# A two-layer graph network with a gated feed-forward block: how the two edge passes are drained into the stages behind them

## The chip, the cores and the metric

The kernel runs on one core of one Trainium2 chip, in one launch. The metric is device time in microseconds; a kernel's time is the median of its runs. One more execution of each kernel is profiled, and all rows below come from that one.

## The reference

`x` is [20000, 512] in float32; `src` and `dst` are 10,000 edges, `dst` sorted. `LN` is a layer norm without weights.

```python
xl = (h @ Wl + bl).reshape(N, 4, 128); xr = (h @ Wr + br).reshape(N, 4, 128)
logits = einsum('ehc,hc->eh', leaky_relu(xl[src] + xr[dst], 0.2), att)   # edges and self loops
p = exp(logits - segment_max(logits, dst)[dst]); alpha = p / segment_sum(p, dst)[dst]
layer(h) = segment_sum(xl[src] * alpha, dst) + bias
x = x + layer1(elu(layer0(LN(x))))
x = x + ffn(LN(x))      # a gate averaged over all rows merges eight sets of weights, then two products
```

A node without an edge only has its self loop, so its row comes from the dense product. Nodes with edges are worked out in the edge pass and written over the dense rows afterwards.

## The kernel before

Seven stages follow each other: `transform_first` (layer norm, the first dense product), `edge_pass` for layer 0, `transform_second` (ELU and the second dense product), `edge_pass` for layer 1, `gate` (residual, layer norm, the gate's product), `merge` and `ffn`. The dense stages go through 157 tiles of 128 nodes. The edge passes go through T = 79 tiles of edges, which are grouped for the softmax into eight groups of 9 tiles, one of 4 and one of 3. `edge_pass` and the stage behind it share a block, so no barrier stands between them: each engine goes on to the next stage when its own list for the edge pass is through.

Every engine runs its own instructions in the order of the code, and semaphores tie the engines together. In the helpers `pipeline(n, [(step, ahead), ...])`, loop turn k runs `step(k + ahead)`.

The change is about the end of each edge pass, called the drain here. In it

- ScalarE weighs the edges' feature rows by their shares (`weigh`), a tile's two halves into `w1` and `w2`; the odd tiles among the last nine (71, 73, 75, 77: the list `helped`) are weighed by VectorE (`weigh_too`);
- for the last nine tiles, 70 to 78, TensorE adds the two halves in a bank of PSUM by two products with the identity (`add_near`); earlier tiles are added by a DMA;
- VectorE runs the sum along the edges, tile after tile (`accumulate`: `acc[t] = acc[t-1] * same + added`, four instructions of 128 columns where a group begins, at 72 and 76), and SyncE stores every tile to the table `touched`;
- VectorE picks each partition's first end out of `top` and `total` (20 copies and a product into `picked`, then a reduction). These stand between the sums of tiles 75 and 76;
- segments that cross partitions are joined: VectorE and ScalarE form shares, TensorE transposes them and multiplies them with the last sum, GpSimd fetches the rows to be completed (`row_fetched`), VectorE scales and adds them, GpSimd scatters them back (`join_stored`).

After `join_stored` GpSimd fetches, node tile by node tile, the edge results over the dense rows (`fetch_over`). SyncE has loaded these dense rows before: up to 12 tiles ahead in `transform_second` (`VR`), and up to 9 ahead in `gate` (`GX`), where the tile of `x` is loaded with them. A fetch waits for its tile's load. ScalarE's list for `transform_second` starts with three loads: two vectors, and the next root weights `Wr1` (1 MB).

Of the kernel before, what the change touches and what calls it, by code (L numbers as in the profile page):

```python
# [10 lines left out]
ALU = mybir.AluOpType  # L11
# [3 lines left out]
P = 128  # L15
D = 512
H = 4
# [11 lines left out]
G = 9  # L29
LAST = (4, 3)  # L30
CATCH = 30
TAIL = 9
LEAD = 7
R = 18
OWN, SRC = 0, 1
# [4 lines left out]
AR = 6  # L40
# [17 lines left out]
def need(eng, sem, value):  # L58

    if value > 0:  # L60
        eng.wait_ge(sem, value)
# [512 lines left out]
def edge_signals(nc, c, layer):  # L574

    return group(nc, c, f"e{layer}", "w_loaded w_high w_low b_loaded chain ready transposed featT root z leaky product product_own logit "
              "bottom exps shares weighted weighted_too near_added summed trail_set trail_stored others_loaded "
              "share_exps share_sums share_in share_T share_copied shared joined cleared",
              stored=AR)


def edge_pass(nc, layer, g, s, block):
# [25 lines left out]
    def columns(buf, i):  # L608
        a, b = span(i)
        return heads(buf[:, a:b])  # L610
# [27 lines left out]

    helped = [t for t in range(T - TAIL, T) if t % 2]

    def helped_to(t):
        return len([q for q in helped if q <= t])

    def need_weights_free(eng, t):

        if t - WR < near:
            need(eng, s["summed"], t - WR + 1)
        else:
            eng.wait_ge(s["near_added"], t - WR - near + 1)

    def due(k, at):
        return [t for t in range(T) if at[t] == k]
# [1 line left out]
    with ExitStack() as c:  # L654
# [134 lines left out]
        def _(dve):  # L789
            linked = 0  # L790

            def link(ins):
                nonlocal linked
                linked += 1
                ins.then_inc(s["chain"], 1)
                dve.wait_ge(s["chain"], linked)
# [82 lines left out]
            def accumulate(t):  # L879
                b = t % WR  # L880
                if t < near:
                    dve.wait_ge(w_added[b // 2], w0[b // 2] + 16 * (t // WR + 1))
                    added = w1[:, b, :]
                else:
                    dve.wait_ge(s["near_added"], t - near + 1)
                    added = psN[t % 3][:, :]
                need(dve, s["stored"][t % AR], 16 * (t // AR))
                if t == 0:
                    dve.tensor_copy(acc[:, 0, :], added).then_inc(s["summed"], 1)
                elif group_of[t] == group_of[t - 1]:  # L890
                    dve.wait_ge(s["summed"], t)
                    dve.scalar_tensor_tensor(acc[:, t % AR, :], acc[:, (t - 1) % AR, :], same[:, t:t + 1], added,
                                             ALU.mult, ALU.add).then_inc(s["summed"], 1)
                else:
                    carried = columns2(lg, group_of[t])[:, SRC, :, 0]
                    dve.wait_ge(s["summed"], t)
                    for h in range(H):
                        last = dve.scalar_tensor_tensor(acc[:, t % AR, h * C:(h + 1) * C], acc[:, (t - 1) % AR, h * C:(h + 1) * C],
                                                        carried[:, h:h + 1], added[:, h * C:(h + 1) * C], ALU.mult, ALU.add)
                    last.then_inc(s["summed"], 1)  # L900
# [23 lines left out]

            for k in range(T, steps - 2):
                sum_and_weigh(k)
            for i, n in enumerate(sizes):
                dve.tensor_copy(picked[:, 0, :, first[i]:first[i] + n], columns(top, i)[:, :, 1:])
                last = dve.tensor_copy(picked[:, 1, :, first[i]:first[i] + n], columns(total, i)[:, :, 1:])
            link(last)  # L930
            link(dve.tensor_tensor(picked.rearrange("p a h t -> p (a h) t"), picked.rearrange("p a h t -> p (a h) t"),
                                   first_end[:, :].unsqueeze(1).to_broadcast([P, 2 * H, T]), ALU.mult))
            link(dve.tensor_reduce(picked2[:, :, :], picked, AX.X, ALU.add))
            mine = picked2
            for k in range(steps - 2, steps):
# [31 lines left out]
        @block.tensor  # L967
        def _(pe):
            def transposes(t):
                u = t % R  # L970
                pe.wait_ge(got[u], got0[u] + 32 * (t // R + 1))
                need(pe, s["featT"], t - 1)
                for cc in range(KC):
                    last = pe.transpose(psT[t % 2][:, cc * P:(cc + 1) * P], ring[:, u, 0, cc * P:(cc + 1) * P], ident[:, :])  # L974
                last.then_inc(s["transposed"], 1)

            def roots(t):
                b = t % 2
                pe.wait_ge(s["featT"], t + 1)
                need(pe, s["z"], t - 1)  # L980
                for cc in range(KC):
                    pe.matmul(psR[b][:, :], nT[:, b, cc, :], wr[:, cc, :], start=(cc == 0), stop=False)  # L982
                if t == 0:
                    pe.wait_ge(s["ready"], 1)
                pe.matmul(psR[b][:, :], bias_ones[:, :], root_bias[:, :], start=False, stop=True).then_inc(s["root"], 1)  # L985

            def add_near(t):
                b = t % WR
                pe.wait_ge(s["weighted"], t + 1 - helped_to(t))
                need(pe, s["weighted_too"], helped_to(t))  # L990
                if t >= near + 3:
                    pe.wait_ge(s["summed"], t - 2)
                pe.matmul(psN[t % 3][:, :], ident[:, :], w1[:, b, :], start=True, stop=False)
                pe.matmul(psN[t % 3][:, :], ident[:, :], w2[:, b, :], start=False, stop=True).then_inc(s["near_added"], 1)

            pipeline(T, [(transposes, 5), (roots, 4)])
            for t in range(near, T):
                add_near(t)
            pe.wait_ge(s["share_sums"], 1)
            for h in range(H):  # L1000
                last = pe.transpose(psW[:, h * P:(h + 1) * P], weigh_s[:, h, :], ident[:, :])
            last.then_inc(s["share_T"], 1)
            pe.wait_ge(s["share_copied"], 1)
            pe.wait_ge(s["summed"], T)
            for h in range(H):
                last = pe.matmul(psA[:, h * C:(h + 1) * C], share_T[:, h, :], acc[:, (T - 1) % AR, h * C:(h + 1) * C],
                                 start=True, stop=True)
            last.then_inc(s["shared"], 1)
# [23 lines left out]
def transform_second(nc, g, s, block):  # L1032
# [7 lines left out]
    def size(t):  # L1040
        return P if t < n_full else n_rest

    with ExitStack() as c:
# [12 lines left out]
        @block.sync  # L1056
        def _(sp):
            def load(t):
                r, u = size(t), t % VR
                need(sp, s["features"], t - VR + 1)  # L1060
                sp.dma_start(vin[0:r, u, :], before[t * P:t * P + r, 1, :]).then_inc(s["loaded"][u], 16)

            def store(t):
                r, u = size(t), t % VR
                sp.wait_ge(s["left"], t + 1)
                sp.dma_start(table[t * P:t * P + r, :, :], row[0:r, u, :, :]).then_inc(s["stored"][u], 16)

            pipeline(n_tiles, [(load, 11), (store, 0)])
            for u in range(VR):
                sp.wait_ge(s["stored"][u], 16 * len(range(u, n_tiles, VR)))  # L1070
# [10 lines left out]
        @block.scalar  # L1081
        def _(act):
            act.dma_start(g["shift"][1][:, :], bcast(w["bl1"])).then_inc(s["vectors_loaded"], 16)
            act.dma_start(add_bias[:, :], bcast(w["bias1"])).then_inc(s["vectors_loaded"], 16)
            act.dma_start(g["wr"][:, :, :], weight_view(w["Wr1"])).then_inc(s["wr_loaded"], 16)

            def exps(t):
                r, b = size(t), t % 4
                act.wait_ge(s["negative"], t + 1)
                act.activation(mn[0:r, b, :], mn[0:r, b, :], ACT.Exp).then_inc(s["exps"], 1)  # L1090

            def high(t):
                r, b = size(t), t % 3
                act.wait_ge(s["transposed"], t + 1)
                need(act, s["multiplied"], t - 2)
                act.copy(hi[:, b, :, 0:r], chunks(psT[b][:, :])[:, :, 0:r]).then_inc(s["high"], 1)  # L1096

            pipeline(n_tiles, [(high, 4), (exps, 7)])
            act.wait_ge(s["wr_loaded"], 16)

        @block.vector
# [68 lines left out]
def gate(nc, g, inputs, s, block):  # L1170
# [15 lines left out]
    with ExitStack() as c:  # L1186
# [20 lines left out]
        def _(sp):  # L1207
            def load(t):
                r, u = size(t), t % GX
                need(sp, s["x1"], t - GX + 1)  # L1210
                sp.dma_start(vin[0:r, u, :], before[t * P:t * P + r, 1, :]).then_inc(s["loaded"][u], 16)
                sp.dma_start(xin[0:r, u, :], x[t * P:t * P + r, :]).then_inc(s["loaded"][u], 16)
# [431 lines left out]
```

## Time and profile before

| | us |
|---|---|
| median of 3 runs (2934.32 to 2935.56) | 2934.91 |
| the profiled execution | 2934.97 |
| its span | 2933.2 |
| TensorE busy in the span | 2650.6 (90%) |
| VectorE busy | 2510.4 (86%) |
| ScalarE busy | 1478.7 (50%) |
| GpSimd busy | 1225.0 (42%) |

Times in rows are microseconds from the start of the span. A timeline row gives start, duration from the first start to the last end, engine, line, operation, what it writes and reads, and the count of instructions merged in it; in brackets stand the engine's idle time before it and what ended it. PE is TensorE, DVE VectorE, ACT ScalarE, POOL GpSimd, SP SyncE. A product in float32 leaves two matmul records.

### The profile page before, as it was taken

The page shows a single profiled execution, that of the slowest core. Times are in us where ns is not written, and L with a number is a line of the kernel's source. Part 1 is how long each engine was busy: PE and PEld are TensorE (multiplying, and loading weights), DVE is VectorE, ACT ScalarE, POOL GpSimd, SP SyncE. Part 2 cuts the span into 40 slices and gives each one's busy share as a digit, 9 for nine tenths or more (in the row PEclk, how much of TensorE's full clock was granted, in tenths as well). Part 3 has the DMA queues.
Part 4 walks back from the last instruction along what each step waited for, and adds up shares of the span by engine and source line. Part 5 has one row for each costly group of instructions (what it writes and reads, how often), then busy time and mean ns, then how long its engine had stood idle before and what let it go on. Part 6 is the DMA issues. An engine that isn't in the chain of part 4 may idle for free. (4 is left out here: it accounts for less than half of the span.)

```text
span 2933.2 us, 39841 instructions
## 1 busy us (share of the span) xinstructions
PE 2650.6 (90%) x11251; PEld 1805.9 (62%) x11251; DVE 2510.4 (86%) x5399; ACT 1478.7 (50%) x3557; POOL 1225.0 (42%) x1122
## 2 busy tenths in 40 slices
PE   6999999799898499999998989865999999879997
PEld 5777777443343288888873433323888888756665
DVE  7989998699999766776657999997999999379998
ACT  3545545255555333333321655554888888435554
POOL 0012220478886233333317888843333333024444
PEclk8999999899999699999998999986999999889999
DMA  8989999678887688887756888868999999379999
GB/s 323 342 308 321 320 317 347 217 209 248 246 253 218 187 268 277 269 268 265 264 202 197 234 249 251 247 181 297 368 353 349 348 340 347 119 199 252 252 248 172
DMA packets 318998, 782.31 MB, mean 267 GB/s; under 512 B 53584, under 2 KB 54128, under 8 KB 308570
## 3 DMA queue, kind: packets, MB, share of 16 engines
q1 hardware_dynamic: 220152, 539.68, 52.6%
q0 software_dynamic: 96176, 236.29, 32.3%
q10 hardware_dynamic: 2452, 3.79, 0.4%
q8 instruction: 93, 1.52, 0.2%
q14 instruction: 125, 1.02, 0.1%
HBM read 468.08 MB, written 328.75 MB: 272 GB/s over the span
## 5 line engine op out<-in xcount | busy, mean ns | idle before, releaser
L982 PE MATMUL bank<-wr,nT_e 128*128 128x512 f32 x1264 | 592.2, 613 | 71.6 <-DVE z_e L816 60.8
L1157 PE MATMUL bank<-whi,t_hi 128*128 128x512 f32 x1256 | 522.1, 416 | 23.4 <-DVE t_lo L419 23.4
L1159 PE MATMUL bank<-whi,t_lo 128*128 128x512 f32 x1256 | 499.6, 398 | 0.0
L1158 PE MATMUL bank<-wlo,t_hi 128*128 128x512 f32 x1256 | 498.5, 397 | 0.0
L982 PEld LDWEIGHTS bank<-wr,nT_e 128*128 128x128 f32 x1264 | 234.4, 196 | 326.6 <-issue 281.3
L1021 POOL DMA_INDIRECT vin<-touched,node_slot x157 | 167.4, 1066 | 326.2 <-DMA vin<-rows 302.6
L1021 POOL DMA_INDIRECT g_vin<-touched,node_slot x157 | 170.4, 1085 | 318.6 <-DMA g_xin<-in_x 294.0
L1157 PEld LDWEIGHTS bank<-whi,t_hi 128*128 128x128 f32 x1256 | 238.1, 190 | 73.1 <-issue 16.6
L711 POOL DMA_INDIRECT ring_e<-rows,dst_row x158 | 209.3, 1324 | 169.5 <-POOLq L85 134.5
L1159 PEld LDWEIGHTS bank<-whi,t_lo 128*128 128x128 f32 x1256 | 237.2, 189 | 56.3
L1158 PEld LDWEIGHTS bank<-wlo,t_hi 128*128 128x128 f32 x1256 | 238.6, 190 | 45.8
L1352 PE MATMUL bank<-g_hi,whi 128*128 128x512 f32 (+1 forms) x640 | 265.7, 415 | 0.0
L1096 ACT CAST t_hi<-bank 128x512 fp32r<-128x512 f32 (+1 forms) x157 | 91.9, 585 | 329.9 <-PE bank L1159 329.8
L1519 POOL DMA_DIRECT2D out<-f_y x157 | 135.7, 864 | 293.1 <-DVE f_y L1555 290.2
L1354 PE MATMUL bank<-g_lo,whi 128*128 128x512 f32 (+1 forms) x640 | 253.3, 396 | 0.0
L1353 PE MATMUL bank<-g_hi,wlo 128*128 128x512 f32 (+1 forms) x640 | 251.6, 393 | 0.0
L1125 DVE TENSOR_TENSOR t_lo<-bank,t_hi 128x512 fp32r<-128x512 f32 (+1 forms) x157 | 108.2, 689 | 156.6 <-PE bank L1159 156.6
L726 POOL TENSOR_TENSOR z_e<-z_e,v_att 128x512 f32<-128x512 f32 x158 | 203.1, 1285 | 92.8 <-DVE z_e L822 92.0
L754 ACT COPY nT_e<-bank 128x512 f32<-128x512 f32 x158 | 91.5, 579 | 269.0 <-PE bank L974 269.0
L309 POOL DMA_INDIRECT ordered<-pair,place x79 | 76.8, 972 | 354.7 <-DVE place L471 354.7
L769 ACT ACTIVATE w_e<-ring_e,lg_e 128x128 f32<-128x128 f32 x600 | 191.1, 391 | 61.3 <-DVE lg_e L868 25.2
L816 DVE TENSOR_TENSOR z_e<-bank,ring_e 128x1024 f32<-128x1024 f32 x158 | 191.8, 1214 | 19.2 <-PE bank L985 13.3
(250 smaller groups left out, 5906.8 us busy)
## 6 DMA issues: line engine op xcount, KB each, us to landing
rows<-t_row SPq DMA_DIRECT2D x312, 512.0 KB, 3.8
touched<-acc_e SPq DMA_DIRECT2D x158, 256.0 KB, 4.3
xin<-in_x SPq DMA_DIRECT2D x156, 256.0 KB, 4.6
xTin<-in_xT SPq DMA_DIRECT2D x156, 256.0 KB, 3.5
vin<-rows SPq DMA_DIRECT2D x156, 256.0 KB, 3.9
g_vin<-rows SPq DMA_DIRECT2D x156, 256.0 KB, 5.8
g_xin<-in_x SPq DMA_DIRECT2D x156, 256.0 KB, 6.4
out<-g_shifted SPq DMA_DIRECT2D x156, 256.0 KB, 6.3
```

What stands on the lines that cost most here:

```text
L711: pool.indirect_dma_start(ring[:, u, 0:2, :].rearrange("p a d -> p (a d)"), None, whole, bass.IndirectOffsetOnAxis(g["dst_row"][:, t:t + 1 ...
L726: pool.tensor_tensor(z[:, b, 0, :], z[:, b, 0, :], att[:, :], ALU.mult).then_inc(s["product_own"], 1)
L769: act.activation(w1[:, b, h * C:(h + 1) * C], ring[:, u, 2, h * C:(h + 1) * C], ACT.Copy, scale=share_of(lg, SRC, t, h))
L816: dve.tensor_tensor(z[:, b, :, :], psR[t % 2][:, :].unsqueeze(1).to_broadcast([P, 2, D]), ring[:, u, 1:3, :], ALU.add).then_inc(s["z"], 1)
L982: pe.matmul(psR[b][:, :], nT[:, b, cc, :], wr[:, cc, :], start=(cc == 0), stop=False)
L1021: pool.indirect_dma_start(to, None, g["touched"][layer][:, :], bass.IndirectOffsetOnAxis(g["node_slot"][0:r, t:t + 1].bitcast(U32), 0), bo ...
L1157: pe.matmul(ps, hi[:, cc, :], whi[:, cc, :], start=(cc == 0), stop=False)
L1158: pe.matmul(ps, hi[:, cc, :], wlo[:, cc, :], start=False, stop=False)
L1159: last = pe.matmul(ps, lo[:, cc, :], whi[:, cc, :], start=False, stop=(cc == KC - 1))
L1352: pe.matmul(psG[cc][:, 0:n], whi[:, k, cols], hi[:, b, k, 0:n], start=(k == 0), stop=False)
L1353: pe.matmul(psG[cc][:, 0:n], wlo[:, k, cols], hi[:, b, k, 0:n], start=False, stop=False)
L1354: last = pe.matmul(psG[cc][:, 0:n], whi[:, k, cols], lo[:, b, k, 0:n], start=False, stop=(k == KC - 1))
```

## The change

It has six parts.

1. TensorE adds only the tiles that ScalarE weighs (70, 72, 74, 76, 78). For the four that VectorE weighs, VectorE adds `w1` in the running sum and then `w2` in a second instruction (a new semaphore, `half_summed`, stands between the two). TensorE's three banks now turn over the added tiles alone.
2. Behind its last root product TensorE runs 8 products of the identity and `wr` into a bank that is not read (`WARM`).
3. Three products per side take the place of the ten copies per side and the one product over both.
4. `transform_second`'s loads wait: the first for `row_fetched`, and each from tile 6 on until tile t - 6 has been fetched over.
5. `gate`'s loads wait in the same way, with 5 tiles for 6.
6. `Wr1` is loaded at tile 20 of `transform_second` and no longer at its start.

```diff
+WARM = 8
...
+    def added_by_pe(t):
+        return t - near + 1 - helped_to(t)
+
     def helped_to(t):
         return len([q for q in helped if q <= t])
 
     def need_weights_free(eng, t):
 
-        if t - WR < near:
+        if t - WR < near or t - WR in helped:
             need(eng, s["summed"], t - WR + 1)
         else:
-            eng.wait_ge(s["near_added"], t - WR - near + 1)
+            eng.wait_ge(s["near_added"], added_by_pe(t - WR))
...
+                elif t in helped:
+                    dve.wait_ge(s["weighted_too"], helped_to(t))
+                    added = w1[:, b, :]
                 else:
-                    dve.wait_ge(s["near_added"], t - near + 1)
-                    added = psN[t % 3][:, :]
+                    dve.wait_ge(s["near_added"], added_by_pe(t))
+                    added = psN[added_by_pe(t) % 3][:, :]
...
+                    last = dve.scalar_tensor_tensor(acc[:, t % AR, :], acc[:, (t - 1) % AR, :], same[:, t:t + 1], added,
+                                                    ALU.mult, ALU.add)
+                    if t in helped:
+                        last.then_inc(s["half_summed"], 1)
+                        dve.wait_ge(s["half_summed"], helped_to(t))
+                        last = dve.tensor_tensor(acc[:, t % AR, :], acc[:, t % AR, :], w2[:, b, :], ALU.add)
+                    last.then_inc(s["summed"], 1)
...
-            for i, n in enumerate(sizes):
-                dve.tensor_copy(picked[:, 0, :, first[i]:first[i] + n], columns(top, i)[:, :, 1:])
-                last = dve.tensor_copy(picked[:, 1, :, first[i]:first[i] + n], columns(total, i)[:, :, 1:])
+            whole_groups = sizes.count(G)
+            for side, buf in enumerate((top, total)):
+                n = whole_groups * G
+                dve.tensor_tensor(picked[:, side, :, 0:n].rearrange("p h (i t) -> p i h t", i=whole_groups),
+                                  buf[:, 0:H * (n + whole_groups)].rearrange("p (i h t) -> p i h t", i=whole_groups, h=H)[:, :, :, 1:],
+                                  first_end[:, 0:n].rearrange("p (i t) -> p i t", i=whole_groups).unsqueeze(2).to_broadcast(
+                                      [P, whole_groups, H, G]), ALU.mult)
+                for i in range(whole_groups, NC):
+                    at, n = first[i], sizes[i]
+                    last = dve.tensor_tensor(picked[:, side, :, at:at + n], columns(buf, i)[:, :, 1:],
+                                             first_end[:, at:at + n].unsqueeze(1).to_broadcast([P, H, n]), ALU.mult)
             link(last)
-            link(dve.tensor_tensor(picked.rearrange("p a h t -> p (a h) t"), picked.rearrange("p a h t -> p (a h) t"),
-                                   first_end[:, :].unsqueeze(1).to_broadcast([P, 2 * H, T]), ALU.mult))
...
+                b, ps = t % WR, psN[added_by_pe(t) % 3]
                 pe.wait_ge(s["weighted"], t + 1 - helped_to(t))
-                need(pe, s["weighted_too"], helped_to(t))
-                if t >= near + 3:
-                    pe.wait_ge(s["summed"], t - 2)
-                pe.matmul(psN[t % 3][:, :], ident[:, :], w1[:, b, :], start=True, stop=False)
-                pe.matmul(psN[t % 3][:, :], ident[:, :], w2[:, b, :], start=False, stop=True).then_inc(s["near_added"], 1)
+                if t >= near + 6:
+                    pe.wait_ge(s["summed"], t - 5)
+                pe.matmul(ps[:, :], ident[:, :], w1[:, b, :], start=True, stop=False)
+                pe.matmul(ps[:, :], ident[:, :], w2[:, b, :], start=False, stop=True).then_inc(s["near_added"], 1)
...
+            for _ in range(WARM):
+                pe.matmul(psN[0][:, :], ident[:, :], wr[:, 0, :], start=True, stop=True)
             for t in range(near, T):
-                add_near(t)
+                if t not in helped:
+                    add_near(t)
@@ transform_second: load(t)
+                if t == 0:
+                    sp.wait_ge(g["row_fetched"], 16)
+                if t >= 6:
+                    sp.wait_ge(replaced[(t - 6) % VR], replaced0[(t - 6) % VR] + 16 * ((t - 6) // VR + 1))
@@ transform_second: ScalarE
-            act.dma_start(g["wr"][:, :, :], weight_view(w["Wr1"])).then_inc(s["wr_loaded"], 16)
+
+            def root_weights(t):
+                if t == 20:
+                    act.dma_start(g["wr"][:, :, :], weight_view(w["Wr1"])).then_inc(s["wr_loaded"], 16)
@@ gate: load(t)
+                if t == 0:
+                    sp.wait_ge(g["row_fetched"], 32)
+                if t >= 5:
+                    sp.wait_ge(replaced[(t - 5) % GX], replaced0[(t - 5) % GX] + 16 * ((t - 5) // GX + 1))
```

On VectorE, from the sum of tile 70 of layer 0 to the first pick, the order before was (`acc_e` is the running sum, `bank` a bank of PSUM, `w_e` is `w1` or `w2`, `nT_e` holds `picked`):

```order
L892 SCALAR_TENSOR_TENSOR acc_e<-acc_e,same,bank 128x512 [waits e0_summed,e0_stored4,e0_near_added]
L892 SCALAR_TENSOR_TENSOR acc_e<-acc_e,same,bank 128x512 [waits e0_summed,e0_stored5,e0_near_added]
L898 SCALAR_TENSOR_TENSOR acc_e<-acc_e,lg_e,bank 128x128 [waits e0_summed,e0_stored0,e0_near_added]
L898 SCALAR_TENSOR_TENSOR acc_e<-acc_e,lg_e,bank 128x128 x3
L892 SCALAR_TENSOR_TENSOR acc_e<-acc_e,same,bank 128x512 [waits e0_summed,e0_stored1,e0_near_added]
L876 TENSOR_TENSOR w_e<-ring_e,lg_e 128x512 [waits e0_near_added,e0_shares]
L877 TENSOR_TENSOR w_e<-ring_e,lg_e 128x512
L892 SCALAR_TENSOR_TENSOR acc_e<-acc_e,same,bank 128x512 [waits e0_summed,e0_stored2,e0_near_added]
L892 SCALAR_TENSOR_TENSOR acc_e<-acc_e,same,bank 128x512 [waits e0_summed,e0_stored3,e0_near_added]
L928 COPY nT_e<-top_e 128x4x9
```

In the changed kernel the same place, up to the reduction of the picks, reads:

```order
L899 SCALAR_TENSOR_TENSOR acc_e<-acc_e,same,w_e 128x512 [waits e0_summed,e0_stored3,e0_weighted_too]
L904 TENSOR_TENSOR acc_e<-acc_e,w_e 128x512 [waits e0_half_summed]
L942 TENSOR_TENSOR nT_e<-top_e,first_end 128x8x4x9
L948 TENSOR_TENSOR nT_e<-top_e,first_end 128x4x4
L948 TENSOR_TENSOR nT_e<-top_e,first_end 128x4x3
L942 TENSOR_TENSOR nT_e<-total_e,first_end 128x8x4x9
L948 TENSOR_TENSOR nT_e<-total_e,first_end 128x4x4
L948 TENSOR_TENSOR nT_e<-total_e,first_end 128x4x3
L951 TENSOR_REDUCE picked_e<-nT_e 128x8 [waits e0_chain]
```

Each of the four sums over a tile that VectorE weighs now has a second instruction behind it, and 21 instructions ahead of the reduction have become 6.

On TensorE, from the last root product of layer 0 to the first transpose of the join, the changed kernel has:

```order
L1003 MATMUL bank<-root_bias_e,bias_ones 128x512
L1015 MATMUL bank<-wr,ident 128x512 x8
L1010 MATMUL bank<-w_e,ident 128x512 [waits e0_weighted]
L1011 MATMUL bank<-w_e,ident 128x512
...
L1010 MATMUL bank<-w_e,ident 128x512 [waits e0_summed,e0_weighted]
L1011 MATMUL bank<-w_e,ident 128x512
L1021 MATMUL bank<-ident,z_e 128x128 [waits e0_share_sums]
```

There were nine pairs of additions here and are five, with the eight products ahead of them that wait for nothing.

On SyncE, at the start of `transform_second`, twelve loads stood in a row without a wait; now they are:

```order
L1085 DMA vin<-rows 128x512 [waits row_fetched]
L1085 DMA vin<-rows 128x512 x5
L1085 DMA vin<-rows 128x512 [waits gathered0]
L1085 DMA vin<-rows 128x512 [waits gathered1]
L1085 DMA vin<-rows 128x512 [waits gathered2]
```

`gathered0` is the landing of tile 0's fetch. Everything behind a waiting load on SyncE's list, the stores of finished tiles among it, waits with it.

## Rows read from the trace of the kernel before

**Rows 1.** Stretches from A to B: length, engines' busy time (instructions), clock, DMA share, GB/s.

```profile
960.00:1030.00 70.00, 30.94 (x79) 17.29 (x80) 47.49 (x120) 26.70 (x82) 19.24 (x18) 0.63 0.58 186
2045.00:2560.00 515.00, 507.96 (x2507) 417.06 (x2505) 436.85 (x1035) 398.48 (x914) 153.19 (x142) 0.99 0.93 323
```

**Rows 2.** Timeline of VectorE, the end of layer 0's edge pass.

```profile
981.24 1.62 DVE L892 SCALAR_TENSOR_TENSOR acc_e<-acc_e,same,bank 128x512 f32<-128x512 f32 x2
...
985.51 0.68 DVE L877 TENSOR_TENSOR w_e<-ring_e,lg_e 128x512 f32<-128x512 f32 x1
...
987.55 0.75 DVE L892 SCALAR_TENSOR_TENSOR acc_e<-acc_e,same,bank 128x512 f32<-128x512 f32 x1 [0.70 <-PE bank L994]
988.22 0.18 DVE L928 COPY nT_e<-top_e 128x36 f32<-128x36 f32 x1
...
990.05 0.82 DVE L931 TENSOR_TENSOR nT_e<-nT_e,first_end 128x632 f32<-128x632 f32 x1
990.90 0.81 DVE L933 TENSOR_REDUCE picked_e<-nT_e 128x8 f32<-128x632 f32 x1
...
993.00 1.63 DVE L892 SCALAR_TENSOR_TENSOR acc_e<-acc_e,same,bank 128x512 f32<-128x512 f32 x2
```

**Rows 3.** Timeline of TensorE, the same drain and the next stage's first product.

```profile
956.49 0.50 PE L985 MATMUL bank<-root_bias_e,bias_ones 33*128 33x512 f32 x1
973.37 2.08 PE L993 MATMUL bank<-w_e,ident 128*128 128x512 f32 x2 [16.38 <-ACT w_e L771]
...
999.97 1.11 PE L1001 MATMUL bank<-ident,z_e 128*128 128x128 f32 x4 [7.30 <-DVEq L949]
1001.75 2.08 PE L1006 MATMUL bank<-acc_e,z_e 128*128 128x128 f32 x8 [0.67 <-ACT z_e L786]
...
1024.66 0.78 PE L1157 MATMUL bank<-whi,t_hi 128*128 128x512 f32 x1
```

**Rows 4.** Timeline of VectorE, the join of layer 0.

```profile
1001.59 0.16 DVE L955 TENSOR_TENSOR gain_e<-gain_e,scale_e 128x4 f32<-128x4 f32 x1
1004.80 0.88 DVE L958 TENSOR_SCALAR w_e<-w_e,gain_e 128x128 f32<-128x128 f32 x4 [3.05 <-DMA w_e<-touched,join_row]
1005.71 1.12 DVE L963 SCALAR_TENSOR_TENSOR w_e<-bank,scale_e,w_e 128x128 f32<-128x128 f32 x4
```

**Rows 5.** Timeline of GpSimd, layer 0's join and the first fetch.

```profile
997.96 1.10 POOL L738 DMA_INDIRECT w_e<-touched,join_row  x1 [25.80 <-issue]
1007.66 1.07 POOL L742 DMA_INDIRECT touched<-w_e,join_row  x1 [8.60 <-DVE w_e L963]
1013.48 1.03 POOL L1021 DMA_INDIRECT vin<-touched,node_slot  x1 [4.75 <-DMA touched<-w_e,join_row]
```

**Rows 6.** DMA issues from 990 to 1020: KB each, median us to landing.

```profile
vin<-rows SPq DMA_DIRECT2D x12, 256.0 KB, 5.5
...
vin<-touched,node_slot POOLq DMA_INDIRECT x5, 3.5
w_e<-touched,join_row POOLq DMA_INDIRECT x1, 6.7
touched<-w_e,join_row POOLq DMA_INDIRECT x1, 4.9
```

**Rows 7.** Timeline of TensorE, layer 1's join.

```profile
2002.35 2.08 PE L1006 MATMUL bank<-acc_e,z_e 128*128 128x128 f32 x8 [0.67 <-ACT z_e L786]
```

**Rows 8.** Timeline of VectorE, layer 1's join and tile 5 of the gate.

```profile
2005.73 1.13 DVE L963 SCALAR_TENSOR_TENSOR w_e<-bank,scale_e,w_e 128x128 f32<-128x128 f32 x4
...
2027.66 0.68 DVE L1293 TENSOR_TENSOR g_x<-g_xin,g_vin 128x512 f32<-128x512 f32 x1
```

**Rows 9.** Timeline of GpSimd, the gate's first fetch.

```profile
2013.77 1.03 POOL L1021 DMA_INDIRECT g_vin<-touched,node_slot  x1 [5.04 <-DMA touched<-w_e,join_row]
```

**Rows 10.** DMA issues in the gate, 2050 to 2550.

```profile
g_xin<-in_x SPq DMA_DIRECT2D x136, 256.0 KB, 6.4
...
g_vin<-touched,node_slot POOLq DMA_INDIRECT x139, 6.1
```

More of the change, by code:

```diff
@@ L576, in edge_signals @@
     return group(nc, c, f"e{layer}", "w_loaded w_high w_low b_loaded chain ready transposed featT root z leaky product product_own logit "
-              "bottom exps shares weighted weighted_too near_added summed trail_set trail_stored others_loaded "
+              "bottom exps shares weighted weighted_too near_added half_summed summed trail_set trail_stored others_loaded "
               "share_exps share_sums share_in share_T share_copied shared joined cleared",
@@ L891, in accumulate @@
                     dve.wait_ge(s["summed"], t)
-                    dve.scalar_tensor_tensor(acc[:, t % AR, :], acc[:, (t - 1) % AR, :], same[:, t:t + 1], added,
-                                             ALU.mult, ALU.add).then_inc(s["summed"], 1)
+                    last = dve.scalar_tensor_tensor(acc[:, t % AR, :], acc[:, (t - 1) % AR, :], same[:, t:t + 1], added,
[5 more added lines that the diff above has]
+                    last.then_inc(s["summed"], 1)
                 else:
@@ L987, in add_near @@
             def add_near(t):
-                b = t % WR
+                b, ps = t % WR, psN[added_by_pe(t) % 3]
                 pe.wait_ge(s["weighted"], t + 1 - helped_to(t))
-                need(pe, s["weighted_too"], helped_to(t))
-                if t >= near + 3:
-                    pe.wait_ge(s["summed"], t - 2)
-                pe.matmul(psN[t % 3][:, :], ident[:, :], w1[:, b, :], start=True, stop=False)
-                pe.matmul(psN[t % 3][:, :], ident[:, :], w2[:, b, :], start=False, stop=True).then_inc(s["near_added"], 1)
+                if t >= near + 6:
+                    pe.wait_ge(s["summed"], t - 5)
+                pe.matmul(ps[:, :], ident[:, :], w1[:, b, :], start=True, stop=False)
+                pe.matmul(ps[:, :], ident[:, :], w2[:, b, :], start=False, stop=True).then_inc(s["near_added"], 1)
             pipeline(T, [(transposes, 5), (roots, 4)])
+            for _ in range(WARM):
+                pe.matmul(psN[0][:, :], ident[:, :], wr[:, 0, :], start=True, stop=True)
             for t in range(near, T):
-                add_near(t)
+                if t not in helped:
+                    add_near(t)
             pe.wait_ge(s["share_sums"], 1)
@@ L1096, in high @@
                 act.copy(hi[:, b, :, 0:r], chunks(psT[b][:, :])[:, :, 0:r]).then_inc(s["high"], 1)
-            pipeline(n_tiles, [(high, 4), (exps, 7)])
+            pipeline(n_tiles, [(high, 4), (exps, 7), (root_weights, 0)])
             act.wait_ge(s["wr_loaded"], 16)
```

## The prediction

> **What bounds the kernel now.** I read the windows first, then VectorE's and TensorE's timelines at the end of an edge pass, then GpSimd's timeline and the DMA issues between two stages, and last the same places in layer 1. The windows give two kinds of stretch. In the gate's steady part TensorE is busy 507.96 of 515 us, so only TensorE's own work counts there, and a shift of its first product passes on to the end of the stage [rows 1]. In the drain of layer 0 no engine is near full: TensorE 30.94 of 70 us, VectorE 47.49, the DMA engines 0.58 [rows 1]. There a chain sets the time. From 956.99, when the last root product ends (956.49 + 0.50), to 1024.66, the first product of the next stage, TensorE is not the limit [rows 3]. VectorE is, nearly without a gap, to the end of its last sum at 994.63 (993.00 + 1.63) [rows 2]. Behind it come the row fetch at 997.96, TensorE's join products, ending 1003.83, VectorE's completion at 1005.71, the scatter at 1007.66 and the first fetch at 1013.48 [rows 3 to 5]. Both drains have this form (completion at 1005.71 and 2005.73, first fetch at 1013.48 and 2013.77) [rows 4, 5, 8, 9].
>
> **VectorE's four additions (part 1).** Two dependent sums take 1.63 for 2 x 0.75, so a dependent instruction starts 0.13 after the one before it [rows 2]. An addition of 512 columns is like the product L877, 0.68 [rows 2]. Four cost 4 x (0.68 + 0.13) = +3.24 a drain. Bounds: 4 x 0.59 = 2.4, if each overlaps its neighbour as the picks do (0.18 long, 0.09 apart: 20 of them from 988.22 to 990.05), and 4 x 0.88 = 3.5 at the price of a sum. In return the wait of 0.70 for TensorE's bank goes [rows 2], of which 0.13 would stay: -0.57. What is late next there is VectorE itself. The eight matmuls that TensorE loses were awaited nowhere else, so they bring nothing more.
>
> **The eight products (part 2).** At the slowest rate that the rows show, 2.08 for a float32 product of 512 columns (L993), they end at 956.99 + 16.6 = 973.6, against a first addition at 973.37, which waits for ScalarE [rows 3]. VectorE takes that bank only at 981.24 [rows 2]: the cost is 0. I also give them no gain. Behind 7.30 us of idling the transposes L1001 (256 columns in 1.11) run at the same slow rate as L993 behind 16.38, the lower of the two levels, in a stretch with a mean granted clock of 0.63 [rows 1, 3]; and nothing that stands in front of the additions shortens the idling in front of L1001.
>
> **The picks (part 3).** Before: 988.22 to 990.90, 2.68 [rows 2]. The slope between 512 and 632 columns is (0.82 - 0.68) / 120 = 1.17 ns a column [rows 2], so 288 columns take 0.42. Two of these less 0.09 of overlap, four small ones at 0.09 and a dependent gap give 0.66 + 0.36 + 0.13 = 1.15; I take 1.2, a saving of 1.48. Bounds: 0.9, if it costs what the one product over 632 columns does (0.82 and a gap), and 1.9, if nothing overlaps: 2 x (0.42 + 0.13) + 4 x 0.18.
>
> Parts 1 and 3 together make VectorE's end 3.24 - 0.57 - 1.48 = **+1.2** later (bounds +0.05 and +2.15), so the last sum ends at about 995.8.
>
> **The loads in the first drain (parts 4 and 6).** The row fetch took 6.7 beside twelve loads of 256 KB and `Wr1`'s 1 MB, while the small fetches of the same stretch took 3.5 [rows 6]. Now it has the queues to itself: issued at 999.16, landed at 1002.66. VectorE is ready for it at 1001.59 + 0.16 + 1.2 = 1002.95 and has scaled the rows by 1003.83 [rows 4]. TensorE's join products end at 1003.83 + 1.2 = 1005.03 [rows 3]. So TensorE is late next, and the completion starts at 1005.16, 0.13 behind it: **-0.55** (bounds -1.70 and +0.40, with VectorE's bounds). The wait of 3.05 for the DMA [rows 4] is worth this little because VectorE's later end uses up most of it. The scatter follows the completion by 1.12 + 0.83: 1007.11. The six released loads of 256 KB start at 1002.7, land 5.5 later, and overlap its start: I put its landing at 3.6 for 4.9 [rows 5, 6], **-1.3** (bounds 0 and -1.4). First fetch at 1007.11 + 3.6 + 0.92 = 1011.6. Behind it the loads from tile 6 on share the queues with the fetches of tiles 1 to 5. That was no neighbour before: **+0.4**, bounds 0 and +2.6, from 3.5 [rows 6] to the 6.1 that a fetch takes in a full stage [rows 10]. First drain: **-1.45**, bounds -3.1 and +3.0. What waits behind a waiting load on SP are later loads and the stores of finished tiles; no one in the stage waits for these. In the steady part a load has six tiles of lead and is the only one of its tile, so I cost it by the tighter case, the gate, at 0. `Wr1` at tile 20 is 1 MB, 3.2 us of DMA at 323 GB/s [rows 1], hidden by the same lead; 3.2 is its price without it.
>
> The Trainium skill, "DMA: Bandwidth & Descriptors", section "Queues, rings and completion order", says that each DMA engine goes round between the queues that have work, packet by packet. By that a fetch of GpSimd would not stand behind the whole list of SP's loads. The row of 6.7 against 3.5 agrees only in part: the fetch did not wait for 3 MB to pass, which at the stretch's 186 GB/s [rows 1] would take 16 us, but it took twice its quiet time. By the rule the saving at the scatter would shrink towards 0, since only loads in flight count, and the sum would be 1.3 higher.
>
> **The loads in the second drain (part 5).** TensorE's join products end at 2002.35 + 2.08 + 1.2 = 2005.63 [rows 7], the completion starts at 2005.76 against 2005.73 [rows 8]: **0** (bounds -1.1 and +1.0). Five tiles of two loads, 2.6 MB, are released near 2002.7, and at 323 GB/s [rows 1] flow for 8 us, until 2010.8, past the scatter at 2007.7. Its landing gains **-0.4**; bounds 0 and -1.7 (the wait for it was 5.04 for the 4.75 of layer 0 [rows 5, 9], so about 5.2, down to 3.5). Then comes tile 5, whose loads are issued only when tile 0's fetch has landed. From a first fetch at F: 3.5, then 5.5 for the load, 0.9 to the next fetch, 3.5 for it: F + 13.4; with the gate's 6.4 and 6.1 [rows 10] F + 16.9. VectorE wants tile 5 at F + 13.9 (2027.66 - 2013.77) [rows 8, 9]. With 0.5 for two issues and some sharing I put the stall at **+0.9**, bounds 0 and +3.0. Second drain: **+0.5**, bounds -2.8 and +4.0. In the steady gate the round of a buffer is 6.4 + 0.9 + 6.1 = 13.4 [rows 10] against five tiles of 515 / 157 = 3.28 each (2507 records, 16 a tile) [rows 1], 16.4: it fits, with 3.0 to spare.
>
> **Sum.** -1.45 + 0.5 = -0.9. The profiled execution took 2934.97, 1.77 more than its span, and lies 0.06 above the median of 2934.91, so no correction is due: **2934.1**, by the bounds 2929.1 to 2942.0.
>
> **Rivals.**
> A, faster: transfers alone set the drains. VectorE's end moves by 0.05 only, both scatters land in a quiet 3.5, and no ramp stalls: the low bounds, -3.1 - 2.8 = -5.9, **2929.1**. For it: the 3.05 of waiting for the row fetch, the longest stall of the join. Against it: it needs additions that overlap, though each waits for the sum before it.
> B, slower: the gate's loop of five tiles takes over from TensorE. It decides once load, pick-up and fetch take 16.4 in the mean, 3.0 above the sum of the medians. A loop of 16.8 is 0.08 a tile, +12 over 150 tiles: **2946**. For it: the DMA engines are 0.93 busy there [rows 1], landings scatter about a median, and SP issues in order, so one late fetch holds the loads and stores behind it. Against it: fewer loads in flight should land sooner.
> C: the late loads cost the ramps their high ends, 2.6 and 3.0 in place of 0.4 and 0.9: +4.3, **2938.4**. The Trainium skill, "DMA: Bandwidth & Descriptors", section "Rules for kernel authors", advises to issue a DMA early and to wait for it late, which speaks against parts 4 and 5; the steady 13.4 against 16.4 says that here the rule bites in the ramps alone.
> D: the clock stays up through the join, so L1001 and L1006 (1.11 + 2.08) take half, -1.6 on TensorE's path; VectorE's scaled rows at 1003.83 then cap it at -1.2 a drain: **2931.7**.
>
> **How the numbers follow.** A measurement can tell about 0.2% from no change, 5.9 us: "same" is 2929.0 to 2940.8. Chances: the forecast 0.57 (0.02 faster, 0.53 same, 0.02 slower), A 0.22 with its like, of which 0.13 falls below 2929.0 since it lies at that edge, B 0.14, all slower, C 0.04 (0.03 same, 0.01 slower), D 0.03 (0.02 faster, with part of A, 0.01 same). That makes 0.17 faster, 0.66 same, 0.17 slower. The range is 2927.5 to 2943.0: the bounds, stretched a little below for A; what is left out is most of B and the far end of A.
>
> **What would show it.** VectorE: the last sum of layer 0 ends near 995.8, and L958 has no wait for a DMA. TensorE's L1006 ends near 1005.0 and is what VectorE's completion waits for. The scatter lands in about 3.6, the first fetch comes at 1011.6 and 2013.4, the first product of the second transform at 1023.2. The first addition still runs at the lower clock. It is wrong if the gate's steady part shows TensorE waiting for fetched tiles (B), or if VectorE's end stays at 994.7 (A).

## The result: 0.15% slower

| | us |
|---|---|
| before, median of 20 runs (2932.53 to 2938.4) | 2935.14 |
| changed, median of 20 runs (2938.2 to 2944.73) | 2939.6 |
| ratio, 95% interval | 1.0015 (1.0009 to 1.0021) |
| span of the profiled execution, before and changed | 2933.2, 2937.3 |

The time lies in the range, but the kernel became 4.5 slower and not 0.9 faster. The windows of the changed kernel, with the columns of [rows 1], show the same two kinds of stretch: no engine is near full in the drain, and TensorE bounds the gate.

```profile
960.00:1030.00 70.00, 28.08 (x70) 14.99 (x69) 48.67 (x108) 26.66 (x81) 18.30 (x18) 0.66 0.54 172
2045.00:2560.00 515.00, 512.13 (x2522) 419.46 (x2520) 441.15 (x1044) 401.65 (x920) 154.62 (x144) 0.99 0.94 330
```

The difference is in the drains. VectorE's timeline there, against [rows 2, 4]:

```profile
989.33 0.69 DVE L904 TENSOR_TENSOR acc_e<-acc_e,w_e 128x512 f32<-128x512 f32 x1
989.94 0.45 DVE L942 TENSOR_TENSOR nT_e<-top_e,first_end 128x288 f32<-128x288 f32 x1
...
991.13 0.81 DVE L951 TENSOR_REDUCE picked_e<-nT_e 128x8 f32<-128x632 f32 x1
...
994.84 0.75 DVE L899 SCALAR_TENSOR_TENSOR acc_e<-acc_e,same,bank 128x512 f32<-128x512 f32 x1
...
1002.75 0.87 DVE L976 TENSOR_SCALAR w_e<-w_e,gain_e 128x128 f32<-128x128 f32 x4
1004.90 1.12 DVE L981 SCALAR_TENSOR_TENSOR w_e<-bank,scale_e,w_e 128x128 f32<-128x128 f32 x4 [1.28 <-PE bank L1026]
```

The picks take 1.19 (989.94 to 991.13), the last sum ends at 995.59, and the completion waits for TensorE (L1026) and for no DMA. On TensorE, against [rows 3], the eight products end at 964.14, the first addition still runs at the lower clock, and the stage's first product is 0.74 later:

```profile
957.01 7.13 PE L1015 MATMUL bank<-wr,ident 128*128 128x512 f32 x16
973.47 2.08 PE L1010 MATMUL bank<-w_e,ident 128*128 128x512 f32 x2 [9.32 <-ACT w_e L775]
...
1002.72 2.08 PE L1026 MATMUL bank<-acc_e,z_e 128*128 128x128 f32 x8 [0.68 <-ACT z_e L790]
...
1025.40 0.78 PE L1184 MATMUL bank<-whi,t_hi 128*128 128x512 f32 x1
```

GpSimd's timeline and the DMA issues from 990 to 1020, against [rows 5, 6]:

```profile
998.83 1.10 POOL L742 DMA_INDIRECT w_e<-touched,join_row  x1 [26.57 <-issue]
1006.85 1.07 POOL L746 DMA_INDIRECT touched<-w_e,join_row  x1 [6.92 <-DVE w_e L981]
1012.82 1.03 POOL L1041 DMA_INDIRECT vin<-touched,node_slot  x1 [4.89 <-DMA touched<-w_e,join_row]
```

```profile
vin<-rows SPq DMA_DIRECT2D x9, 256.0 KB, 6.0
...
vin<-touched,node_slot POOLq DMA_INDIRECT x6, 4.3
w_e<-touched,join_row POOLq DMA_INDIRECT x1, 3.2
touched<-w_e,join_row POOLq DMA_INDIRECT x1, 5.0
```

The row fetch fell from 6.7 to 3.2, but the scatter went from 4.9 to 5.0 and the first fetches from 3.5 to 4.3. In the gate, against [rows 8, 9], VectorE waits at two tiles behind the first (the third and the sixth), GpSimd's sixth fetch waits for a load released late, and the first product comes at 2045.00 (2040.70 before; 2.1 of these 4.3 are there already when the second drain begins):

```profile
2019.49 0.69 DVE L1324 TENSOR_TENSOR g_x<-g_xin,g_vin 128x512 f32<-128x512 f32 x1 [3.40 <-DMA g_vin<-touched,node_slot]
...
2023.52 0.69 DVE L1324 TENSOR_TENSOR g_x<-g_xin,g_vin 128x512 f32<-128x512 f32 x1 [0.30 <-DMA g_vin<-touched,node_slot]
...
2031.96 0.69 DVE L1324 TENSOR_TENSOR g_x<-g_xin,g_vin 128x512 f32<-128x512 f32 x1 [1.56 <-DMA g_vin<-touched,node_slot]
```

```profile
2009.50 1.06 POOL L746 DMA_INDIRECT touched<-w_e,join_row  x1 [6.92 <-DVE w_e L981]
2016.04 1.04 POOL L1041 DMA_INDIRECT g_vin<-touched,node_slot  x1 [5.49 <-DMA touched<-w_e,join_row]
...
2025.23 1.51 POOL L1041 DMA_INDIRECT g_vin<-touched,node_slot  x1 [2.66 <-DMA g_xin<-in_x]
```

A third place was not thought of: TensorE's first eight root records of layer 1's edge pass, first in the kernel before, then in the changed one:

```profile
1553.00 4.60 PE L982 MATMUL bank<-wr,nT_e 128*128 128x512 f32 x8
```

```profile
1553.63 6.05 PE L1000 MATMUL bank<-wr,nT_e 128*128 128x512 f32 x8
```

The same work, but the clock rises later in it: at the lower of its two levels a record starts 0.85 after the one before it, at the higher 0.43, and the changed kernel runs more of the eight at the lower.

### The profile page after: what moved, and what is told of

It reads as the page before. It is cut to its first block and busy times, and to the rows that moved or that the text cites. A ratio compares the mean times of both kernels' runs of the same rounds, so it can differ in the third digit from the quotient of the medians.

```text
span 2937.3 us, 40102 instructions
## 1 busy us (share of the span) xinstructions
PE 2659.4 (91%) x11251; PEld 1806.9 (62%) x11251; DVE 2514.8 (86%) x5377; ACT 1481.3 (50%) x3557; POOL 1226.3 (42%) x1122
## 5 line engine op out<-in xcount | busy, mean ns | idle before, releaser
L1000 PE MATMUL bank<-wr,nT_e 128*128 128x512 f32 x1264 | 600.3, 619 | 65.1 <-DVE z_e L820 54.1
```

## The experiments

All are read by three spans: drain 0 and drain 1, from the end of the last root product to the first product of the next dense stage, and the fill of layer 1's edge pass, from its first transpose to its first finished root product. Each is one profile, but for means over four profiles of the kernel before and three of the changed one. Ratios are each against the kernel before, timed beside that run.

| | ratio (95%) | drain 0 | drain 1 | fill |
|---|---|---|---|---|
| before, mean of 4 | | 67.57 | 83.14 | 8.31 |
| changed, mean of 3 | 1.0015 (1.0009-1.0021) | 68.25 | 84.67 | 9.56 |
| adds | 1.0015 (1.0006-1.0024) | 69.94 | 85.86 | 9.03 |
| picks | 0.9989 (0.9980-0.9998) | 66.07 | 82.04 | 9.14 |
| late_loads | 0.9998 (0.9989-1.0007) | 67.05 | 85.40 | 9.09 |
| no_late_loads | 1.0016 (1.0007-1.0025) | 68.45 | 84.00 | 9.40 |
| no_warm | 1.0017 (1.0008-1.0026) | 68.07 | 85.21 | 9.34 |
| first_wait_only | 1.0014 (1.0005-1.0023) | 68.68 | 85.44 | 9.29 |
| early_a | 1.0003 (0.9994-1.0012) | 67.51 | 86.47 | 8.79 |
| early_b | 1.0020 (1.0011-1.0029) | 71.70 | 86.16 | 9.07 |
| pool_early | 1.0002 (0.9993-1.0011) | 66.98 | 84.29 | 9.41 |
| pool_early_alone | 1.0010 (1.0001-1.0019) | 67.08 | 85.83 | 9.44 |

The profiles of one kernel differ among themselves. The four of the kernel before lie between 66.85 and 68.57 in drain 0 (the last from a profile whose last sum ended 1.7 later than in the other three) and between 82.76 and 83.60 in drain 1; the three of the changed one between 68.10 and 68.32, and 84.34 and 84.92. So the changed kernel's +1.5 in drain 1 is clear of this spread, and its +0.7 in drain 0 is not by itself.

**One part alone.** The first is part 1, the second part 3, the third parts 4 to 6, the fourth parts 1 to 3, each with its lines of the diff above on the kernel before.

```diff
 # adds
...
+                        last = dve.tensor_tensor(acc[:, t % AR, :], acc[:, t % AR, :], w2[:, b, :], ALU.add)
...
```

> Part 1 alone on the kernel before: VectorE adds the four tiles it weighs. Both theories: the four additions cost 4 x 0.81 less the stall of 0.57 to 0.70, so VectorE's last sum ends 2.4 to 2.6 later in each drain; the row fetch still stands beside the loads and moves with it, so +2.5 a drain, +5.0, 2940. If instead the wait for the row fetch hides it (the fetch is issued behind the last store, so I do not expect it), 0.

Measured 1.0015, drains +2.4 and +2.7 over the mean: as expected.

```diff
 # picks
-            for i, n in enumerate(sizes):
-                dve.tensor_copy(picked[:, 0, :, first[i]:first[i] + n], columns(top, i)[:, :, 1:])
+            whole_groups = sizes.count(G)
...
```

> Part 3 alone: six products for the 20 copies and one product. The profile of the changed kernel shows 1.19 for 2.68, so VectorE's last sum ends 1.5 earlier in each drain, and the row fetch, completion and scatter with it: -3.0, 2932. If the loads, issued behind the last store and so also 1.5 earlier, set the landing of the row fetch and the scatter, it is still -1.5 a drain; if the transfers of the stage do not move, 0.

Measured 2933.13 against 2936.88, drains -1.5 and -1.1, both below all four of the kernel before: it passes on. This is the one part that is faster, and the best kernel of all that ran, though the upper end of its interval is only just below 1.

```diff
 # late_loads
+                if t == 0:
+                    sp.wait_ge(g["row_fetched"], 16)
...
```

> Parts 4 to 6 alone: the loads are released late, VectorE and TensorE as before. Theory 1 (the late loads are the cost): the completion comes 1.3 to 1.75 earlier, but the scatter lands no sooner and the first tiles behind it are late (second transform +1.0 to 1.3, gate +1.6 to 1.9 at tile 5 and +0.4 on the scatter): +0.5 to +1.5, 2935.6 to 2936.6, and the stall of VectorE before tile 5 of the gate is there. Theory 2 (VectorE's later end is the cost): the late loads gain, -1.5 a drain, 2932.

The ratio holds both (-3.2 to +2.1 us); the profile decides for theory 1 in the second drain (+2.3), while the first gains 0.5, which is inside the spread. GpSimd's rows of the first drain show why it is no more: the completion is early (46.96 behind the last root product, 48.79 before), but the scatter behind it still takes 5.2 to land.

```profile
997.60 1.11 POOL L738 DMA_INDIRECT w_e<-touched,join_row  x1 [25.68 <-issue]
1005.64 1.07 POOL L742 DMA_INDIRECT touched<-w_e,join_row  x1 [6.93 <-DVE w_e L963]
1011.78 1.03 POOL L1021 DMA_INDIRECT vin<-touched,node_slot  x1 [5.06 <-DMA touched<-w_e,join_row]
```

```diff
 # no_late_loads: the changed kernel without
-                if t == 0:
-                    sp.wait_ge(g["row_fetched"], 16)
...
-                if t == 20:
```

> Parts 1 to 3 alone, the loads and Wr1 as before. Theory 1: VectorE's last sum ends 0.9 later in each drain and the row fetch with it: +1.8, 2937, and no stall in the gate's tile 5. Theory 2: +4, 2939, as much as the whole change.

1.0016 is nearer theory 2, but the drains are theory 1: +0.9 each, and no tile behind the first waits in the gate. With the fill (9.40, +1.1) this comes to +2.8, inside the interval (from +2.1 us up). By the times alone, parts 1 to 3 cost as much as the whole change and the late loads nothing. By the drains, both together, parts 1 to 3 cost 1.7 and the late loads add 0.5. The single parts 1 and 3 would add up to 1.0004, and their intervals are too wide to tell that from 1.0016.

**The eight products.**

```diff
 # no_warm: the changed kernel without
-            for _ in range(WARM):
-                pe.matmul(psN[0][:, :], ident[:, :], wr[:, 0, :], start=True, stop=True)
```

> The changed kernel without the eight products behind the last root product. Theory that they do nothing (the first addition runs at the same 2.08 with them and without): 2939.6, drains 68.3 and 84.9 within 0.5. Rival, that they cost something that the kernels with parts 1 to 3 show beyond the sum of parts 1 and 3: 2936 to 2937.

1.0017 against the changed kernel's 1.0015, and the first addition takes 2.07 without them for 2.08 with them: no effect is seen, at an interval of 0.0009 either way.

**The release tile by tile, or the traffic.**

```diff
 # first_wait_only: the changed kernel without
-                if t >= 6:
-                    sp.wait_ge(replaced[(t - 6) % VR], replaced0[(t - 6) % VR] + 16 * ((t - 6) // VR + 1))
...
```

> The changed kernel with only the first load of a stage waiting for the row fetch; the waits tile by tile are out, so 12 and 9 tiles of loads follow at once. If the release tile by tile is the cost (a fetch, then a load, then a fetch in a row before tile 5 of the gate), VectorE's 1.56 before that tile goes and the stage's first product comes 1.5 earlier, though the scatter beside 18 loads lands later by up to 1.5: 2937 to 2939. If what costs is that loads flow beside the scatter and the first fetches, the scatter takes 6 to 7 instead of 5.6 and the fetches over 4.5, and the time stays at 2939.5 or goes above it.

Both halves came true and nearly cancel. No tile of the gate behind the first waits, but the scatter lands in 6.4 where twelve loads are released and in 6.9 where eighteen are (gate, issues from 2006 to 2040), and the first product comes no sooner: the drains are 0.4 and 0.8 longer than the changed kernel's.

```profile
touched<-w_e,join_row POOLq DMA_INDIRECT x1, 6.9
```

**Loads ahead of the last stores, on SP.**

```diff
 # early_a (early_b: 12 and 6 for 6 and 4)
+            for t in range(6):
+                load(t)
+            g["rest_of_stores"]()
+            sp.wait_ge(g["join_stored"], 16)
...
```

> The kernel before with part 3 and Wr1 at tile 20, and the loads moved the other way: 6 tiles of the second transform and 4 of the gate are loaded ahead of the last three stores of the edge pass (as soon as all tiles are weighed), the others after the join's scatter has landed. The row fetch should take 3.2, the completion come 3 earlier than before. Theory that the scatter pays for loads beside it: it lands in 3.5 to 4, first fetches 4 earlier, about -3.5 a drain: 2928. Rival, that the scatter takes its 4.7 to 5 by itself: about -3 a drain, 2929 to 2930. If the loads behind the join spoil the first tiles as in the changed kernel: +1.5 to 2 a drain of it, 2932.

> As the one with 6 and 4 tiles ahead, with 12 and 6 tiles. Then the second transform has no load beside its first fetches, which keep 3.4 each, and the gate fewer: 1.4 less in the first drain and up to 1 in the second than with 6 and 4, 2926 to 2928. Rival: the issue of 12 loads holds up the last three stores, so that the row fetch comes up to 1 later: no better than with 6 and 4.

Both gains were real and were lost elsewhere. With no load beside it the scatter lands in 2.6, against 4.3 to 6.9 in every run with loads beside it; GpSimd's rows of early_a, first drain:

```profile
998.90 1.10 POOL L747 DMA_INDIRECT w_e<-touched,join_row  x1 [27.60 <-issue]
1005.42 1.07 POOL L751 DMA_INDIRECT touched<-w_e,join_row  x1 [5.42 <-DVE w_e L978]
1008.99 1.03 POOL L1036 DMA_INDIRECT vin<-touched,node_slot  x1 [2.50 <-DMA touched<-w_e,join_row]
```

The first fetch follows the last root product (956.13) by 52.9, 3.3 sooner than the mean before. But the loads behind the join make the first fetches take 6 to 8, and the last three stores, behind the early loads, land in 5.1 to 6.8, so that in the second drain the row fetch is issued 45.3 behind the last root product for 40.2. In early_b the last three stores stand behind twelve loads on SP's queue, land late, and the row fetch is issued 50.3 behind the last root product for 41.4 (its median for a store was 2.0):

```profile
touched<-acc_e SPq DMA_DIRECT2D x5, 256.0 KB, 6.4
```

**The same loads from GpSimd's queue, earlier.**

```diff
 # pool_early (pool_early_alone: without part 3)
+            for t in range(VR):
+                pool.dma_start(vin[:, t, :], before[t * P:(t + 1) * P, 1, :]).then_inc(g["ahead0"], 16)
+            g["join_fetch"]()
...
```

> The kernel before with part 3 and Wr1 at tile 20, and all first loads of the two stages (12, and 9 pairs) issued by GpSimd as soon as the tiles up to 69 are weighed, near 972, in buffers that lie over rows already weighed. GpSimd idles there, and the stores stay alone in SP's queue, which in the runs with 6 and 12 tiles ahead on SP stood behind the loads (row fetch 3 and 10 later). Theory (the loads cost wherever they meet the join or the first fetches): row fetch 3.2, completion 3 earlier than before, scatter 2.6, first fetches 5 to 5.5 earlier, no late tile: -4 to -5 a drain, 2925 to 2928. Rival, that loads beside the last stores hold these up on the shared DMA engines just as well: row fetch issued later than 39.8 behind the last root product, and no better than part 3 alone, 2932 to 2934.

> As the run with GpSimd's early loads, without part 3: tells how much of it is the loads. 1.5 a drain slower than with it if VectorE's last sum still sets the row fetch: 2928 to 2931; 0 to 0.5 if TensorE or a transfer sets the completion.

The rival came true, and the time is above that of part 3 alone. In the first drain the scatter takes 2.6 and the first fetches 3.5, but the stores now land in 5.4, and the running sum, which has six buffers, waits for them. Without part 3 (1.0010) the sum waits in the same place, and the drains are 0.1 and 1.5 longer than with it. VectorE in pool_early, the sum of tile 75:

```profile
994.25 0.75 DVE L896 SCALAR_TENSOR_TENSOR acc_e<-acc_e,same,bank 128x512 f32<-128x512 f32 x1 [3.60 <-DMA touched<-acc_e]
```

**The kernels themselves once more** (again, again_2 and again_3 are the kernel before; changed_2 and changed_3 the changed one).

> The kernel before once more, for its profile and as the measure of how far equal kernels lie apart. Theory that the start of layer 1's edge pass, 8.1 from its first transpose to its first finished root product in the profile of before and 9.0 to 9.5 in all others, depends on the moment at which the clock rises and not on the change: it lies somewhere in 8 to 9.5 here too. If it belongs to the changes: 8.1 again. Drains 67.7 and 82.8 as before; time within 0.1%.

> The kernel before, one more profile. If the moment at which the clock rises belongs to the single execution, the start of layer 1's edge pass takes anything from 8.1 to 9.5 here; if to the kernel, 8.1 as in the two others. Drains near 67.4 and 83.2.

> The kernel before, a fourth profile. As for the third: 8.1 at the start of layer 1's edge pass if that belongs to the kernel, else anything from 8.1 to 9.5; drains near 67.4 and 83.2.

> The changed kernel, one more profile. If the moment at which the clock rises belongs to the single execution, the start of layer 1's edge pass takes anything from 8.1 to 9.5; if to the kernel, 9.5 again. Drains near 68.3 and 84.9.

> The changed kernel, a third profile. As for the second: 9.5 at the start of layer 1's edge pass if that belongs to the kernel, else anything from 8.1 to 9.5; drains near 68.3 and 84.9.

`again` timed at 1.0000 (0.9991 to 1.0009). Its fill, and that of the other two, was 8.08, 8.90 and 8.13; of the changed kernel 9.97 and 9.22. So the fill moves between executions of one kernel by up to 0.8, and 8.1 is not the kernel's own. Yet all three fills of the changed kernel lie above all four of the kernel before, and no other kernel came below 8.79. The same stretch of layer 0, measured in the same way, took 8.89 in the mean of either kernel's profiles. What sets the fill stays open.

## Why the prediction was wrong, step by step

Means over the profiles named above; the completion (the start of VectorE's sum L963, in the changed kernel L981) is measured from the last root product's end:

| step | predicted | measured |
|---|---|---|
| first drain: completion | -0.55 | 48.79 to 47.81: -0.98 |
| scatter landing | -1.3 | 4.51 to 5.00: +0.5 |
| first fetch to first product | +0.4 | 11.36 to 12.52: +1.2 |
| second drain: completion | 0 | 48.09 to 47.46: -0.6 |
| scatter landing | -0.4 | 5.21 to 5.96: +0.75 |
| first fetch to first product | +0.9 | 26.93 to 28.34: +1.4 |
| both drains | -0.95 | +2.2 |

- **Parts 1 and 3** were sized nearly right: 1.19 for the picks (1.2 said), and the last sum ends 0.86 later behind the last root product in both drains (1.2 said). That is why the completions came a little earlier than said, and TensorE was what came late next, as written. The 0.86 leaves out the one late profile of the kernel before; without it the -0.98 is -0.65. Alone, the parts cost 0.9 a drain (no_late_loads). Part 2 showed no effect.
- **The step that failed: "I put its landing at 3.6 for 4.9, -1.3", and "its landing gains -0.4".** I took the loads to be nearly gone when the scatter starts. They were not: the six of the first drain were issued one after another from 1002.00 on, 5 to 2 us ahead of the scatter at 1006.85, took 6.8 in the median to land (5.5 from 1002.7 said), and flowed beside it. Nor was the scatter of the kernel before free of traffic: ten of its twelve loads had landed when it was issued, but the 1 MB of `Wr1`, issued at 1002.15, was on its way for 10.0. Part 6 took that load from beside the scatter, and part 4 put five of the six there in its place. SyncE's loads in the changed kernel, `Wr1` in the kernel before, and the window of the scatter before, changed and in early_a (the last number is GB/s):

```profile
1002.00 3.58 SPq L1085 DMA_DIRECT2D vin<-rows  x6
```

```profile
wr<-in_Wr ACTq DMA_DIRECT2D x1, 1024.0 KB, 10.0
```

```profile
1007.66:1012.51 4.85, 0.00 (x0) 0.00 (x0) 0.69 (x1) 0.00 (x0) 1.07 (x1) 0.50 0.66 253
1006.85:1011.85 5.00, 0.00 (x0) 0.00 (x0) 0.69 (x1) 0.00 (x0) 1.07 (x1) 0.50 0.77 291
1005.42:1008.03 2.61, 0.00 (x0) 0.00 (x0) 0.00 (x0) 0.00 (x0) 1.07 (x1) 0.50 0.09 30
```

The runs give the scale: 2.6 with no load beside it (early_a, early_b, pool_early, both drains; so the 3.5 taken as its quiet time was too long), 5.0 with the six loads released in the changed kernel's first drain, 6.0 with the ten of the second, 6.4 and 6.9 with twelve and eighteen. A later release by itself moves the traffic from the row fetch, where TensorE and VectorE hid part of it, to the scatter, where nothing does. This is 2.95 of the 3.15 by which the drains missed; the ramps' +1.3 and the completions' -1.1 nearly cancel. So the 1.7 that parts 1 and 3 cost was not paid back by the loads.

- **The ramps** (first fetch to first product) were mis-sized, 0.4 and 0.9 for 1.2 and 1.4. The mechanism was the one given: in the gate tile 5 waits 1.56 for a load released by tile 0's fetch, and the fetches slow down beside the loads. Rival C, to which I gave 0.04, had this place right; its ends (2.6 and 3.0) were too far.
- **Rival A** failed on VectorE's end (0.86 later and not 0.05) and on the scatter, which it also took to be quiet, **rival B** did not occur (512.1 to 512.3 for the gate's products in all profiles of both kernels), and **D** did not: the join's products take 2.08 as before.
- **Not in the sum:** the fill of layer 1's edge pass, +1.25 in the mean. The profiles do not account for all of the 4.5 between the medians (interval 2.6 to 6.2): their spans differ by 2.7 in the mean (2934.8 and 2937.5). In them the drains' +2.2 and the fill's +1.25 are partly offset by the stretch up to the first drain, 1.2 shorter in the changed kernel's profiles (956.9 to 957.3, against 957.0 to 959.8); the other stretches differ by 0.2 or less. How the rest of the 4.5 divides stays open.

The Trainium skill, "DMA: Bandwidth & Descriptors", section "Queues, rings and completion order", has the DMA engines go round between queues packet by packet. The prediction's reading of it, that only loads in flight count and the saving at the scatter shrinks to 0, agrees with the runs: 5.0 behind a release of six loads, 2.6 with none; the round between the queues itself no run shows. The advice of the Trainium skill, the same page, section "Rules for kernel authors", to issue a DMA early and wait for it late, held for what came behind the early loads (scatter 2.6, first fetches 3.5 in the first drains of early_b and pool_early). It did not pay here: the loads issued early on SP held up the stores behind them, the ones from GpSimd slowed the stores beside them.

The version to keep is part 3 alone: 0.9989 (0.9980 to 0.9998).

## What to carry to other kernels

When a transfer is delayed to clear the way for one that is waited for, ask which waited-for transfer it meets next, and price that one with the same slowdown: here a row fetch went from 6.4 to 3.2 and the completion behind it came 1.0 earlier, and the scatter, issued 5 us behind the release, met the released loads and took 0.5 longer. A store whose buffer is waited for belongs to the chain as much as a load does. Small work taken off the chain itself (the picks, 1.5 and 1.1 in the two drains) passed on, as no reordering of the loads did.

## What was not expected of the hardware

- The indirect scatter of the joined rows lands in 2.6 with no load beside it (the DMA engines moved 30 GB/s, so 0.08 MB, in that time), less than the fetch of the same rows (3.2). It nearly doubles, to 5.0, behind a release of six loads and takes 6.9 with eighteen.
- The moment at which TensorE's clock rises in layer 1's edge pass differs between executions: 5.4 to 8.1 after the first transpose in the seven profiles of the two kernels, for equal work, and the fill from 8.1 to 10.0 (in the profile with 10.0 the first root product also started 0.7 to 0.9 later than in the others).
